# Three pieces of VectorE's edge work in another order, in the graph stage of a two-layer kernel

## The reference

```python
self_feat = vcq @ W_self.T + b_self            # vcq: x, and the condition where a row's sum isn't 0
for d in range(2):
    A = (adj_f if d == 0 else swapaxes(adj_f, 1, 2))[:, :, :20, :]    # 11 labels per edge
    cond = A.sum(-1)                            # count of labels
    vb = A @ w_bias + b_bias                    # label bias
    aff = einsum('bnhd,bmhd->bnhm', qh, kh) * (1.0 / sqrt(dh))
    aff = where(cond > 0, aff, NEG) + vb
    w = softmax(aff, axis=-1)
    output = output + (w @ kv, through Wout) + bout
x = x + relu(output)
```

## Time and profile before

| | |
|---|---|
| median of 3 runs | 830.25 us (828.51 to 830.90) |
| profiled execution | 831.57 us, its span 829.9 us |
| busy: TensorE, VectorE, ScalarE, GpSimd | 754.1, 502.9, 478.8, 346.0 us |
| mean granted TensorE clock | 0.972 |

### The profile page before, as it was taken

One profiled execution on the slowest core, in us unless ns is written; L12 is line 12 of the kernel. 1 busy time (PEld: TensorE's weight loads), 2 busy tenths in 40 slices (PEclk: granted clock), 3 DMA queues, 4 the chain that ended last, 5 costly groups with the idle time before them and its releaser, 6 DMA issues.

```text
span 829.9 us, 15335 instructions
## 1 busy us (share of the span) xinstructions
PE 754.1 (91%) x4800; PEld 547.2 (66%) x4800; DVE 502.9 (61%) x1031; ACT 478.8 (58%) x812; POOL 346.0 (42%) x549
## 2 busy tenths in 40 slices
PE   4798999999997689999999999999878999999997
PEld 2577777777774346666566666556546888888885
DVE  2248999999998755555566666565433534444432
ACT  0324545545544367777777777777655655555543
POOL 1024656556563454555555555554730222222110
PEclk9789999999999789999999999999999999999999
DMA  7821423233210565656556666655600000000001
GB/s 228 292 62 38 123 76 110 77 108 112 86 51 17 114 117 114 116 115 116 115 114 114 114 114 112 117 109 114 121 2 1 1 25 26 26 26 26 15 25 39
DMA packets 84457, 71.09 MB, mean 86 GB/s; under 512 B 22270, under 2 KB 83326, under 8 KB 84414
## 3 DMA queue, kind: packets, MB, share of 16 engines
q1 hardware_dynamic: 83086, 70.38, 37.0%
q10 hardware_dynamic: 1328, 0.16, 0.1%
HBM read 52.94 MB, written 17.43 MB: 85 GB/s over the span
## 4 chain that ended last, share of the span: by engine, by line
PE 47%; ACT 8%; issue 5%; DVE 4%; DMA 2%; POOL 1%; SPq 1%; ACTq 0%; POOLq 0%
PE ps L1633 10%; PE ps L1647 10%; PE ps L1523 5%; PE ps L1509 5%; ACT probsT L873 4%; PE ps L1561 3%; PE ps L1461 3%; PE ps L1453 2%; PE ps L1542 2%; ACT w_ada L902 2%; PE ps L1476 1%; ACT projT L894 1%; DVE qk L1122 1%; DMA parts_dram<-w_ada 1%; PE ps L1445 1%
## 5 line engine op out<-in xcount | busy, mean ns | idle before, releaser
L873 ACT ACTIVATE probsT<-ps 128x1024 f32<-128x1024 f32 x128 | 131.0, 1023 | 47.6 <-PE ps L1509 45.6
L1270 DVE TENSOR_TENSOR hidden_low<-hidden,hidden_high 128x512 fp32r<-128x512 f32 x64 | 46.6, 728 | 107.6 <-ACT hidden_high L984 59.6
L1174 DVE TENSOR_REDUCE neg_max<-ps 128x4 bf16<-128x344 f32 x128 | 64.2, 512 | 57.9 <-PE ps L1476 57.0
L1509 PE MATMUL ps<-q_stack,k_stack 97*128 97x256 bf16 x512 | 78.7, 276 | 8.7 <-ACT probsT L873 6.1
L1509 PEld LDWEIGHTS ps<-q_stack,k_stack 97*128 97x128 bf16 x512 | 42.8, 98 | 65.1 <-ACT probsT L873 29.8
L981 ACT ACTIVATE hidden<-ps,b_fc 128x512 f32<-128x512 f32 x64 | 44.2, 690 | 69.6 <-PE ps L1633 69.5
L1523 PE MATMUL ps<-probsT,v_ones 128*32 128x256 f32 x1024 | 69.4, 389 | 9.6 <-ACT probsT L873 9.5
L1453 PE MATMUL ps<-w_qkv,x1T 128*128 128x512 f32 x128 | 65.0, 632 | 2.8 <-DVE rest L1181 2.8
L664 POOL TENSOR_TENSOR scores<-scores,row_max 128x640 f32<-128x640 f32 x32 | 40.8, 1275 | 61.4 <-DVE row_max L1019 61.4
L1371 PE MATMUL ps<-x_res,w_q 128*128 (+1 forms) x256 | 65.2, 401 | 0.1
L806 ACT ACTIVATE weightT<-ps 80x1024 f32<-80x1024 f32 x32 | 32.7, 1021 | 52.6 <-PE ps L1391 52.6
(11 more groups left out here) (177 smaller groups left out, 1821.3 us busy)
## 6 DMA issues: line engine op xcount, KB each, us to landing
parts_dram<-w_ada SPq DMA_DIRECT2D x96, 128.0 KB
q_stack<-parts_dram SPq DMA_DIRECT2D x96, 128.0 KB, 3.9
k_stack<-parts_dram SPq DMA_DIRECT2D x32, 256.0 KB, 6.3
adj<-in_adj SPq DMA_DIRECT2D x16, 440.0 KB, 3.5
xT<-in_xT SPq DMA_DIRECT2D x16, 256.0 KB, 2.7
x_res<-in_x SPq DMA_DIRECT2D x16, 256.0 KB, 3.5
x_in<-in_x SPq DMA_DIRECT2D x16, 256.0 KB, 2.7
k_stack<-parts_dram SPq DMA_DIRECT2D x32, 128.0 KB, 4.9
```

The costliest lines, as they stand in the source:

```text
L873: nc.scalar.activation(probsT[:, s % 4, :], ps[:, COLS:COLS + 2, :].rearrange("p a n -> p (a n)"), ACT.Exp).then_inc(exp_made, 1)
L1174: nc.vector.tensor_reduce(places[:, :, k], ps[:, ROW_BANKS[n % 2], 0:4 * KP].rearrange("p (a g) -> p a g", a=4), AX_X, ALU.max, negate=Tru ...
L1270: nc.vector.tensor_tensor(hidden_parts[1][:, s % H_SLOTS, :], hidden[:, s % RAW, :], hidden_parts[0][:, s % H_SLOTS, :], ALU.subtract).the ...
L1509: mm = nc.tensor.matmul(ps[:, COLS + j, kt * N:(kt + 1) * N], k_stack[:, par, place, kt * P:(kt + 1) * P], q_stack[:, par, place, :], star ...
```

## The change

VectorE's `label_products` and `label_sums` are split into `edge_labels` (the product), `edge_counts`, `no_edges` and `label_sums` (the reduce), and three of the pieces move within the turn. The product now stands between the first direction's scores and their row_max, `no_edge` between the second direction's row_sum and its reciprocal, and nz_diag in front of mixT.

```diff
-        def graph_scores(b, par, d):
+        def graph_scores(b, par, d, f=None):
...
                     edge_bias[:, par, tt, d, :].unsqueeze(1).broadcast_to([P, H, M]), ALU.add).then_inc(aff_out, 1)
+            if f is not None:
+                edge_labels(f, 1 - par)
             dve.wait_ge(aff_out, T * (2 * b + d + 1))
             nc.vector.tensor_reduce(row_max[:, d], scores[:, par, d], AX_X, ALU.max).then_inc(edge_max, 1)
...
-        def label_products(f, par):
-
+        def edge_labels(f, par):
             dve.wait_ge(adj_in[par], loads(f, par))
-            edges = adj[:, par].rearrange("p (e l) -> p e l", l=L)
-            nc.vector.tensor_reduce(count[:], edges, AX_X, ALU.add).then_inc(cnt_made, 1)
-            nc.vector.tensor_tensor(weighted[:].rearrange("p (e l) -> p e l", l=L), edges,
+            nc.vector.tensor_tensor(weighted[:].rearrange("p (e l) -> p e l", l=L), adj[:, par].rearrange("p (e l) -> p e l", l=L),
                                     w_label[:].unsqueeze(1).broadcast_to([P, E2, L]), ALU.mult).then_inc(lab_w, 1)
 
+        def edge_counts(f, par):
+            nc.vector.tensor_reduce(count[:], adj[:, par].rearrange("p (e l) -> p e l", l=L), AX_X, ALU.add).then_inc(cnt_made, 1)
+
+        def no_edges(f):
+            dve.wait_ge(cnt_made, f + 1)
+            nc.vector.tensor_scalar(no_edge[:], count[:], 0.0, NEG, ALU.is_le, ALU.mult).then_inc(neg_made, 1)
+
         def label_sums(f, par):
-            dve.wait_ge(cnt_made, f + 1)
-
-            nc.vector.tensor_scalar(no_edge[:], count[:], 0.0, NEG, ALU.is_le, ALU.mult).then_inc(neg_made, 1)
             dve.wait_ge(lab_w, f + 1)
...
-        def sums(b, par, d):
+        def sums(b, par, d, f=None):
             dve.wait_ge(weight_exp, 2 * b + d + 1)
             nc.vector.tensor_reduce(total[:, d], scores[:, par, d], AX_X, ALU.add).then_inc(sum_made, 1)
+            if f is not None:
+                no_edges(f)
             dve.wait_ge(sum_made, 2 * b + d + 1)
             nc.vector.reciprocal(inverse[:, d], total[:, d]).then_inc(rec_made, 1)
...
             if b is not None:
-                graph_scores(b, 1 - par, 0)
+                graph_scores(b, 1 - par, 0, f)
+            elif f is not None:
+                edge_labels(f, par)
             if f is not None:
-                label_products(f, par)
+                edge_counts(f, par)
             if b is not None:
                 graph_scores(b, 1 - par, 1)
             if isinstance(f, int) and f in MOMENTS_AT:
                 moments(MOMENTS_AT.index(f))
+            if following(f) is not None:
+                nonzero(following(f))
             if c is not None:
                 take_output(c)
             if b is not None:
                 sums(b, 1 - par, 0)
-            if following(f) is not None:
-                nonzero(following(f))
             if f is not None:
                 label_sums(f, par)
             if b is not None:
-                sums(b, 1 - par, 1)
+                sums(b, 1 - par, 1, f)
+            elif f is not None:
+                no_edges(f)
```

More of the change, by code:

```diff
@@ L1031, in features, with label_sums @@
             nc.vector.tensor_tensor(feat_at(f), halves(ps, 1), cond[:], ALU.add).then_inc(feat_out, 1)
-        def label_products(f, par):
+        def edge_labels(f, par):
             dve.wait_ge(adj_in[par], loads(f, par))
-            edges = adj[:, par].rearrange("p (e l) -> p e l", l=L)
-            nc.vector.tensor_reduce(count[:], edges, AX_X, ALU.add).then_inc(cnt_made, 1)
-            nc.vector.tensor_tensor(weighted[:].rearrange("p (e l) -> p e l", l=L), edges,
+            nc.vector.tensor_tensor(weighted[:].rearrange("p (e l) -> p e l", l=L), adj[:, par].rearrange("p (e l) -> p e l", l=L),
                                     w_label[:].unsqueeze(1).broadcast_to([P, E2, L]), ALU.mult).then_inc(lab_w, 1)
-        def label_sums(f, par):
+        def edge_counts(f, par):
+            nc.vector.tensor_reduce(count[:], adj[:, par].rearrange("p (e l) -> p e l", l=L), AX_X, ALU.add).then_inc(cnt_made, 1)
+        def no_edges(f):
             dve.wait_ge(cnt_made, f + 1)
             nc.vector.tensor_scalar(no_edge[:], count[:], 0.0, NEG, ALU.is_le, ALU.mult).then_inc(neg_made, 1)
+        def label_sums(f, par):
             dve.wait_ge(lab_w, f + 1)
```

## The result

The changed kernel takes 816.43 us (median of 4 runs, 814.19 to 817.94) against 829.38 us of the kernel before (median of its 4 runs, 827.99 to 830.90): a ratio of 0.984, 95% interval 0.9808 to 0.9872. The forecast was 818.5 us, in a range of 814.5 to 824.5. The profiled execution took 816.26 us, its span 814.2.

What follows compares the result with a forecast made beforehand. With VectorE and TensorE nearly full and TensorE waiting on late VectorE, savings of 9.8, 0.8, 1.0 and 0.2 us took the profiled 831.57 to 819.8; the median's 1.3 lower level gave 818.5 us, range 814.5 to 824.5.

Steps and rivals of the forecast that it cites:

- The bound: Graph stage: TensorE becomes the bound at 12.15 us a turn (12.0 to 12.27), with VectorE 1.2 us to spare.
- the moments: Moments of batch 0, in one of the 12 turns: 0.4 us after the change, partly absorbed by VectorE.
- the weights' wait: TensorE's wait for GpSimd's second normalised weights: about 0.46 us in ordinary turns, expected to go.
- No_edge's price is GpSimd's: no_edge's 1.19 us in a turn is waiting behind GpSimd's normalisation; the instruction itself is not slow.
- Its margin at the new place: no_edge, behind the second row sum, starts 0.25 us after GpSimd's normalisation is done.
- Part 1: no_edge moved behind the second row sum: costs 0.1 us there instead of 1.19 in every full turn.
- Part 2: Product moved between first scores and row_max: costs 1.0 instead of 1.3 us; later row_max chain hidden by 0.25.
- Part 3: nz_diag moved before the mixed values: takes 0.28 us off the path behind the first reciprocal; TensorE's wait for it goes.
- The first rival: nz_diag comes after GpSimd's second shift and waits it out: turn 12.95, 828 us; chance 0.06.
- the stretch ahead of the 12 turns: Before the 12 turns: 0.8 us from one turn's lost waits and 1.0 from an earlier start on the ada vectors.
- The ada vectors' term: Start of the first full turn: VectorE reaches the ada vectors earlier, saving 1.0 us.
- The last turn with new edges: Turn bounded by VectorE alone: loses the product's stall and gains one wait for a result, saving 0.2 us.

Runs made afterwards that it cites:

- e3: The kernel before with no_edge alone moved behind the second row sum: 823.62 us, ratio 0.9929.
- e8: The kernel before, order untouched, with no_edge laid out as 5 groups of 16 with gaps: 824.65 us, ratio 0.9932.
- e9: The changed kernel with one more reduce of weighted, result unused, in each VectorE turn behind the features: 816.52 us, ratio 0.9849 to the kernel before.
- e7: The changed kernel with no_edge behind label_bias, in front of the second row sum: 820.10 us, ratio 0.9882 to the kernel before.
- e2: The kernel before with nz_diag alone moved in front of the mixed values: 817.38 us, ratio 0.9851.
- e6: The changed kernel with no_edge put back in front of label_bias: 815.41 us, ratio 0.9838 to the kernel before.
- e1: The kernel before with the product alone moved between the first scores and row_max: 828.63 us, ratio 0.9997.
- e4: The changed kernel with the product put back in its old place: 816.71 us, ratio 0.984 to the kernel before.
- e11: The kernel before with only the neighbours no_edge and nz_diag exchanged: 827.27 us, ratio 0.9973.
- e5: The changed kernel with nz_diag put back behind the first reciprocal: 821.41 us, ratio 0.9921 to the kernel before.

## Why the prediction was right, and where it was not

- **The bound.** Right. The gain stops where TensorE's own turn begins. I gave 12.15 a turn and 146.2 us for the twelve; they took 145.80, and the ordinary ones 12.07 (as from 198.50 to 210.56). The sum is closer than its terms: the moments were taken at 0.4 and cost 1.0 (two turns of 12.90 and 12.23), which makes up for the 0.08 by which the other turns are shorter. Nor do the two waits have the sizes given: the weights' wait, 0.46 and 0.1 for the modelled end in the prediction, is worth 0.35 (12.92 to e3's and e8's 12.57), and nz_diag's, 0.2 there, is worth 0.50 (12.57 to 12.07). That these misses nearly cancel is luck. e9 shows that VectorE has about a microsecond left.
- **No_edge's price is GpSimd's.** Right, shown three ways: 192 ns at the new place, 562 ns with a part of the overlap (e7), 222 ns in another form at the same place and time (e8). The 192 ns are a little more than the 0.15 us forecast, and 0.12 of them lie on the path. Its margin at the new place was given as 0.25 and is 0.22.
- **Part 1, no_edge moved: what was wrong is which move frees it.** The text priced "no_edge behind the second row sum" at 1.09 us a turn and gave nz_diag's move 0.28 on the path. In fact nz_diag's move alone takes the stall away as well (e2), and no_edge's own move adds nothing to it (e6). I had compared no_edge's end with GpSimd's, and not its start: it was 0.12 late because nz_diag's 0.28 stood in front of it. The one short no_edge of the earlier trace rows, in a turn without nz_diag in front, was the hint; I used it only to show that 138 ns is possible. The forecast of the time did not suffer, since the change makes both moves, but that is luck: by the prediction nz_diag's move alone would have won 0.28 a turn, and it won all.
- **Part 2, the product.** Its own price fell as said (1.07 for 1.39), and the delay of the chain behind row_max was hidden as said. It is worth nothing: e1 and e4 give 0.08 and 0.05 us over 12 turns. The sum was not wrong here, since it took TensorE's turn, but the text counted the product's 0.3 among the work that makes VectorE stop being the bound; the loop that set the turn does not hold it.
- **Part 3, nz_diag.** Its place was hidden as said: it comes 0.16 ahead of the second shift, where the rows gave 0.1 to 0.2. The first rival (a whole shift waited for) did not come, though nz_diag does keep GpSimd off for 0.1, and e11's turn 1 shows it standing behind GpSimd for a whole instruction. TensorE's wait for it, which I took at 0.2 a turn, is worth 0.5 in the loop: e3 and e5 keep it and stand at 151.0 instead of 145.8.
- **The smaller terms.** For the stretch ahead of the 12 turns I gave 1.8 us. Taken from turn 1's second raw scores, free of the clock's start, it is 1.02 (25.43 to 24.41). The ada vectors' term was 1.0 and is 0.34 (from those raw scores to VectorE's ada 8.04 before, 7.70 now): the second row sum there waits 0.30 for ScalarE's exponentials, the cover of part 2 that was thin by forecast and is gone in this first turn. The last turn with new edges was to gain 0.2 and gained 0.13 (15.22 to 15.09), which does not show in the 591.6 us behind the 12 turns.
- **The size.** 11.8 was forecast and the medians differ by 13.0, with an interval of the ratio that spans 5 us. The turns and the term ahead of them are 10.17 + 1.02 = 11.2 in the traces. Compared at one mean granted clock (0.976 to 0.978), eight executions of the kernel before, run beside e1 to e4, have a median of 827.9 us and three of the changed kernel one of 816.3: 11.6. By that, most of what is left of 13.0 goes with the clock of the executions that make up the medians, and not with the change.

## What to carry to other kernels

When an instruction's duration ends with another engine's, compare the two starts as well: if it lost by little, moving the work in front of it can be enough, and a shift of 0.28 us was worth a stall of 1.1 here. Then ask for the shape of the instruction before its place: e8 removed the stall without moving anything. And cost a freed stall against the loop that sets the turn, not against an engine's busy time: of two stalls of VectorE here, one was worth 5 us over 12 turns (e3, e8) and the other nothing (e1, e4). The other 5 us came from a wait of TensorE that the view of waits shows as 0.23 us a turn.

## What the runs showed of the hardware that was not expected

- A VectorE tensor_scalar of 80 values in flat form that is issued 0.12 us after a GpSimd instruction on SBUF waits for its end (1266 ns); with the same values written as 5 groups of 16 it does not (222 ns).
- Between nz_diag and GpSimd it works both ways: 0.16 and 0.11 us ahead of GpSimd, nz_diag lengthens GpSimd's instruction from 1.27 to 1.38 and 1.43 us; 0.02 us behind it, nz_diag takes 1.53 us instead of some 0.4 (e11, turn 1).
- A wait of TensorE that the view of waits gives as 0.23 us cost 0.48 from start to start: the modelled end of a matmul lies behind the start of the next (205.99 + 0.60 against 206.43).
- After the same wait of 5 us TensorE stayed at half clock (granted 0.50) for all of 34 to 46 us in one execution and for about half of it in another (0.73 and 0.72), worth 4.5 us by turn 1.
